# A four-layer vision tower: routed tiles in two 64-row halves with an expert each, and wide attention with its values through DRAM

## What is computed

```
# wide attention, on rms_norm(x, norm1_w)
qkv = x @ w_qkv                        # 12 + 3 + 3 heads of 64
q = apply_rope(q, cos, sin); k = apply_rope(k, cos, sin)
scores = jnp.einsum('bhqd,bhkd->bhqk', q, k) / jnp.sqrt(jnp.float32(HD))
attn = jax.nn.softmax(jnp.where(causal, scores, min), axis=-1)
out = jnp.einsum('bhqk,bhkd->bhqd', attn, v) ... @ w_out

# top-2 routed part, E = 16, FF = 384
vals, idx = jax.lax.top_k(jax.nn.softmax(x2d @ w_router, axis=-1), 2)
vals = vals / jnp.sum(vals, axis=-1, keepdims=True)
for e in range(E):
    gate, up = jnp.split(x2d @ w_gate_up[e], 2, axis=-1)
    out = out + combine[:, e:e + 1] * ((silu(gate) * up) @ w_down[e])

# top-1 routed part, 4 experts, H = 768
top = jnp.argmax(x @ Wg + bg, axis=-1)
y = gelu(x @ W1[top] + b1[top]) @ W2[top] + b2[top]
```

## Time and the profile before

| | |
|---|---|
| time, median of three executions (lowest to highest) | 876.16 us (874.68 to 876.18) |
| the profiled execution: time, span, granted clock | 874.83 us, 873.0 us, 0.977 |
| wide attention | 123 to 262 us |
| first routed part: plan and the last weights | 270 to 302 us |
| its tiles | 302.4 to 437.6 us |
| top-1 tiles | 800.6 to 864 us |

### The profile page before, as it was taken

One profiled execution on the slowest core, in us unless ns is written; L12 is line 12 of the kernel. 1 busy time (PEld: TensorE's weight loads), 2 busy tenths in 40 slices (PEclk: granted clock), 3 DMA queues, 4 the chain that ended last, 5 costly groups with the idle time before them and its releaser, 6 DMA issues. The chain is left out here.

```text
span 873.0 us, 16411 instructions
## 1 busy us (share of the span) xinstructions
PE 814.8 (93%) x5930; PEld 583.5 (67%) x5931; DVE 421.1 (48%) x891; ACT 352.8 (40%) x785; POOL 189.9 (22%) x209
## 2 busy tenths in 40 slices
PE   6999989999999899999999879999999999998997
PEld 4666666677775467777658556765678577665775
DVE  5576577788725322222249677772003477722011
ACT  2375544464332023332325665443241545423332
POOL 0561113554400134444300002000000200001332
PEclk9999999999979999999999999999999999989999
DMA  9021100000005877212133001664000055403110
GB/s 314 1 41 26 17 2 1 1 2 1 2 1 157 230 186 206 59 45 47 40 101 90 0 1 31 134 148 127 1 1 1 11 87 109 115 2 113 45 52 31
DMA packets 80141, 56.21 MB, mean 64 GB/s; under 512 B 53254, under 2 KB 73256, under 8 KB 80076
## 3 DMA queue, kind: packets, MB, share of 16 engines
q1 hardware_dynamic: 71644, 41.26, 19.7%
q0 software_dynamic: 4416, 9.84, 4.1%
q10 hardware_dynamic: 4016, 4.23, 1.5%
HBM read 45.96 MB, written 9.35 MB: 63 GB/s over the span
## 5 line engine op out<-in xcount | busy, mean ns | idle before, releaser
L79 PE MATMUL banks<-con 128*128 128x512 f32 (+1 forms) x230 | 103.6, 566 | 3.0 <-DVEq L2268 1.4
L1978 PE MATMUL banks<-moe_wu,moe_xf 96*128 x256 | 89.1, 492 | 1.7 <-ACT moe_xf L2086 0.9
L1978 PEld LDWEIGHTS banks<-moe_wu,moe_xf 96*128 96x128 f32 x256 | 46.0, 189 | 30.0 <-issue 2.2
L79 PEld LDWEIGHTS banks<-con 128*128 128x128 f32 x230 | 43.5, 203 | 31.8 <-issue 28.4
L154 ACT ACTIVATE ln_sq<-x 96x544 f32<-96x544 f32 x32 | 21.0, 656 | 86.3 <-DVE x L146 86.2
L2283 DVE TENSOR_TENSOR moe_hid<-banks,moe_gs 128x384 f32<-128x384 f32 x32 | 17.9, 558 | 76.2 <-PE banks L1978 76.2
L688 PE MATMUL banks<-x,a_wqkv 96*96 96x272 f32 x192 | 48.0, 395 | 0.0
L2140 POOL DMA_INDIRECT moe_xs<-moe_x_rows,moe_taken x32 | 31.4, 981 | 74.8 <-PE banks L1962 53.0
L1216 DVE TENSOR_TENSOR a_kx<-a_k,con 96x1632 f32<-96x1632 f32 x21 | 38.7, 1850 | 8.0 <-ACT a_k L993 7.7
L1181 POOL MEMSET a_q<- 96x60 f32 x3 | 0.4, 147 | 181.8 <-POOLq L2566 91.9
L164 PE MATMUL banks<-ln_sq,con 96*96 96x272 f32 x128 | 35.6, 400 | 4.0 <-ACT ln_sq L154 3.9
(11 more groups left out here) (413 smaller groups left out, 1720.0 us busy)
## 6 DMA issues: line engine op xcount, KB each, us to landing
moe_wu<-in_moe_up SPq DMA_DIRECT2D x16, 576.0 KB, 11.7
f_w<-in_f_e SPq DMA_DIRECT2D x10, 576.0 KB, 8.2
moe_wd<-in_moe_down SPq DMA_DIRECT2D x16, 288.0 KB, 13.0
patch_px<-in_patches SPq DMA_DIRECT2D x4, 768.0 KB, 9.5
a_vt<-a_v_rows SPq DMA_DIRECT2D x72, 36.0 KB
a_v_rows<-a_vtok SPq DMA_DIRECT2D x24, 96.0 KB, 2.1
f_wu<-in_f_up SPq DMA_DIRECT2D x4, 576.0 KB
f_wd<-in_f_down SPq DMA_DIRECT2D x4, 576.0 KB
```

The lines of the kernel that those rows point to most:

```text
L79: self.nc.tensor.matmul(self.ps[bank][:, 0:width], self.ident, self.con[:, 0:width], start=True, stop=True)
L1978: last = nc.tensor.matmul(ps[2 + 2 * p + u][:, 0:BW], xf[0:KU[a], p, a], wu[0:KU[a], bass.ds(e, 1), a, u * BW:(u + 1) * BW].rearrange("p e ...
```

## The change

**Tiles in two halves.** Counts are rounded up to 64 rows (HT), and a tile consists of two 64-row halves, each with its own expert: `tile_expert` has two entries for each tile, and there are 25 tiles in top-2 and 10 in top-1. Each up and down product becomes two products of 64 rows: rows 0 to 63 go by the first half's expert, in place, rows 64 to 127 by a copy of the second half's weights, `up_copy` and `down_copy`, two of each, made by DVE (96x1536 and 128x576 float32; in top-1 97x1536 and 128x1152). In top-2 the copies lie in the room of `env.x` and `env.x2`, now declared 128 partitions wide. TensorE's `up` waits for `up_copied`, `down` for `down_copied`. DVE's `copy_up(i)` reads the expert number, waits for `w_ready` and for the up products of tile i - 2. In top-1, `take_row` becomes two instructions of 64 rows. The rest of the loop is as before, with 128 rows.

**Values through DRAM.** The two value steps of `project` (L1479) become one that makes the values by token: two blocks of 128 tokens by 192 columns, and for the last 16 tokens a block of 32 rows by 96 columns, twice. ScalarE moves them in two pieces to `vtok`; SyncE writes them to `v_rows` in DRAM (four transfers a chunk) and reads them back as `vt` (three a chunk), 18 rows by 16 images by 64 for each head, of which the 18th row has its slot only. `turn_values`, `take_values` and `vs` are gone; NT = 10.

**Router products spread.** In the last chunk the products of `route_early` for one tile stand behind each of the steps 0 to 3 of the first group; of the remaining two, one stands ahead of each of the steps 0 and 1 of the second group. Their waits move ahead of the first group's steps.

```diff
+HT = 64
+MOE_TILES = -(-((2 * T + NE * (HT - 1)) // HT) // 2)
+TOP1_TILES = -(-((T + NX * (HT - 1)) // HT) // 2)
...
-    NT = TQK + 2
+    NT = TQK + 1
...
+            def write_values(c):
+                sp.wait_ge(taken, NT * (c + 1))
+                for u in range(2):
+                    sp.dma_start(v_rows[c, 128 * u:128 * (u + 1)], vtok[:, c % 2, u * D:(u + 1) * D]).then_inc(v_written, 16)
...
+            def read_values(c):
+                sp.wait_ge(v_written, 64 * (c + 1))
+                if c >= 2:
+                    sp.wait_ge(filled, fill_of(GPC * (c - 1) - 1, 5) + 1)
...
                 else:
-                    w, at, rows = (wv, 0, 2 * WD) if t == TQK else (wv, 2 * WD, WD)
...
+                    for u in range(2):
+                        for a in range(2):
+                            nc.tensor.matmul(to[:, u * D:(u + 1) * D], chunk(x2, c)[:, a, 128 * u:128 * (u + 1)], wv[:, a], start=a == 0, stop=a == 1)
+                    for a in range(2):
+                        for m in range(2):
+                            last = nc.tensor.matmul(to[SLOT * m:SLOT * (m + 1), 2 * D:2 * D + HD], chunk(x2, c)[:, a, CW - SLOT:CW],
+                                                    wv[:, a, m * HD:(m + 1) * HD], start=a == 0, stop=a == 1)
...
+                if not more:
+                    pe.wait_ge(router.small_in, 16)
+                    pe.wait_ge(n2.ready, 2 * (c - 1))
                 for u in range(6):
                     weigh(2 * c, u)
                     if more:
                         project(c + 1, 2 + u)
+                    elif u < ROUTED:
+                        env.route_early(pe, router, x2, 0, u, u + 1)
                 if not more:
-                    pe.wait_ge(router.small_in, 16)
                     pe.wait_ge(n2.ready, 2 * c)
-                    env.route_early(pe, router, x2, 0, 0, EARLY)
                 for u in range(6):
+                    if not more and ROUTED + u < EARLY:
+                        env.route_early(pe, router, x2, 0, ROUTED + u, ROUTED + u + 1)
                     weigh(2 * c + 1, u)
...
             def up(i, p):
                 e = expert(i)
                 pe.wait_ge(w_ready, e + 1)
                 pe.wait_ge(x_moved, i + 1)
+                pe.wait_ge(up_copied, i + 1)
...
                     for a in range(2):
-                        last = nc.tensor.matmul(ps[2 + 2 * p + u][:, 0:BW], xf[0:KU[a], p, a],
-                                                wu[0:KU[a], bass.ds(e, 1), a, u * BW:(u + 1) * BW].rearrange("p e f -> p (e f)"),
-                                                start=a == 0, stop=a == 1)
+                        nc.tensor.matmul(ps[2 + 2 * p + u][0:HT, 0:BW], xf[0:KU[a], p, a, 0:HT],
+                                         wu[0:KU[a], bass.ds(e, 1), a, u * BW:(u + 1) * BW].rearrange("p e f -> p (e f)"),
+                                         start=a == 0, stop=a == 1)
+                        last = nc.tensor.matmul(ps[2 + 2 * p + u][HT:RT, 0:BW], xf[0:KU[a], p, a, HT:RT],
+                                                up_copy[p][0:KU[a], a, u * BW:(u + 1) * BW], start=a == 0, stop=a == 1)
...
+            def copy_up(i, p):
+                e = expert(i, 1)
+                dve.wait_ge(w_ready, e + 1)
+                wait(dve, up_ready, i * 2 - 2)
+                V.tensor_copy(up_copy[p], wu[0:KU[0], bass.ds(e, 1)].rearrange("p e a f -> p (e a) f")).then_inc(up_copied, 1)
+
+            def copy_down(i, p):
+                e = expert(i, 1)
+                V.tensor_copy(down_copy[p], wd[:, bass.ds(e, 1)].rearrange("p e j d -> p (e j) d")).then_inc(down_copied, 1)
...
             def body(i, p, ahead):
                 if top2 and ahead >= 1:
                     gate(i + 1, 1 - p)
+                if ahead >= 2:
+                    copy_up(i + 2, p)
                 if not isinstance(i, int) or i >= 1:
                     move_y(i - 1, 1 - p)
+                if ahead >= 1:
+                    copy_down(i + 1, 1 - p)
                 if not top2 and ahead >= 2:
                     take_row(i + 2, p)
```

More of the change, by code:

```diff
@@ L1499, in bank, with weigh @@
                 return ps[6 + n % 2]
-            def turn_values(g):
+            def weigh(g, u):
                 c = g // GPC
-                pe.wait_ge(taken, NT * (c + 1))
-                to = bank(g, 0)
-                for i in range(GI):
-                    last = nc.tensor.transpose(to[0:KS, i * WD:(i + 1) * WD],
-                                               vs[:, c % 2, (g % GPC) * GI + i].rearrange("p g k -> p (g k)"), env.ident[0:WD, 0:WD])
-                last.then_inc(filled, 1)
-            def weigh(g, u):
                 if u == 0:
@@ L1841, in stage_routed_ffn @@
             here = spare[:, K * NR * LISTS * TL:K * NR * (LISTS + 1) * TL].rearrange("p (k t i) -> p k t i", k=K, t=NR)
+            room = [w[:].rearrange("p a t -> p (a t)") for w in env.whole]
+            up_copy = [r[0:HD, 0:2 * FN2].rearrange("p (a f) -> p a f", a=2) for r in room]
+            down_copy = [r[:, 2 * FN2:2 * FN2 + NH * D].rearrange("p (j d) -> p j d", d=D) for r in room]
+            tile_cmp = spare[0:1, K * NR * LISTS * TL:K * NR * LISTS * TL + 2 * TL * E].rearrange("p (i e) -> p i e", e=E)
             at_lane = experts.wd[:, E - 4:E].rearrange("p e j d -> p (e j d)").rearrange("p (k t r) -> p k t r", k=K, t=NR)
@@ L1844, in stage_routed_ffn @@
             bg, b2 = router.bg, router.b2
-            rest = sb("rest", [RT, TL, D])
+            up_copies, down_copies = sb("up_copies", [KU[0], 2, 2, FN2]), sb("down_copies", [128, 2, NH, D])
+            up_copy, down_copy = ([w[:, p] for p in range(2)] for w in (up_copies, down_copies))
+            rest, tile_cmp = sb("rest", [RT, TL, D]), sb("tile_cmp", [1, 2 * TL, E])[:]
             listed, here, at_lane = sb("listed", [RT, K, NR, LISTS, TL]), sb("here", [RT, K, NR, TL]), sb("at_lane", [RT, K, NR, RT])
@@ L1878, in tiles_loop @@
                 body(i, i, 2)
-            with eng.Fori(1, TL // 2 - 2) as it:
+            turns = (TL - 3) // 2
+            with eng.Fori(1, turns) as it:
                 for u in range(2):
                     body(it * 2 + u, u, 2)
-            for i in range(TL - 4, TL):
+            for i in range(2 * turns, TL):
                 body(i, i % 2, min(2, TL - 1 - i))
@@ L2032, in _ @@
             tiles_loop(pe, body)
-            down(TL - 1, 1)
+            down(TL - 1, END)
             if norm_out:
@@ L2308, in _ @@
             tiles_loop(dve, body)
-            move_y(TL - 1, 1)
+            move_y(TL - 1, END)
             def sum_rows(b):
```

128 lines of the change are left out of this document (67 added, 61 removed).

## The result

The changed kernel took **854.97 us** in the median of four executions (849.39 to 856.25), the one before 875.83 (874.68 to 876.18). The ratio is 0.9752 with a 95% interval of 0.9706 to 0.9798. The forecast was 854, with a range of 843 to 872. In a later session on another chip six executions stood at 851.37 to 852.22, at a ratio of 0.9709 (0.9669 to 0.9749). The profiled execution took 856.25 us, span 854.4, clock 0.977; so the two profiles differ by 18.6 us of span, the medians by 20.9.

What follows compares the result with a forecast made beforehand. TensorE, busy 814.8 of 873.0 us, was taken as the bound, with VectorE bounding the changed top-2 loop. Terms -5.7, -8.4, -4.8 and -3.0 sum to -21.9: 874.8 becomes 852.9, on the median's scale 854; range 843 to 872.

Steps and rivals of the forecast that it cites:

- Top-2 tile over VectorE's chain: Top-2 loop: up products, gate, expert-number read, copy, next up products bound a tile at 5.22 us; -5.7 us.
- Halves side by side, 0.25 us a stay: Up and down products: 64-column halves run together at the present rate, plus 0.25 us per stay in half width.
- The copy waits for the gather: Rival, top-2 loop: the up copy cannot run beside POOL's gather, 0.71 us later per tile; 16.3 us more, 870; chance 0.30.
- Early copy: Rival, top-2 loop: expert number read under the gate, copy starts at the gate's end; 11.3 us less, 843; chance 0.13.
- slow copy: Rival, both routed loops: the up copy takes 1.74 us instead of 0.95; 879 us, slower than before; chance 0.05.
- halves in turn: Rival, routed loops: half-width products run one after the other, up products double; about 110 us more, 964; chance 0.03.
- Top-1: Top-1 loop: 10 tiles of 5.68 us for 12 of 5.43, copies hidden with 0.6 us to spare; -8.4 us.
- Attention before the last chunk: Wide attention: value transposes (4.4 us) and one filler (0.4) go, values through DRAM arrive in time; -4.8 us.
- Last chunk: Wide attention's end: spread router products gain 6.0 us if the clock stays up, 0.9 if it falls; middle taken, -3 us.

Runs made afterwards that it cites:

- routed stages alone: The changed kernel's routed stages with the wide attention of the kernel before; 858.1 us, ratio 0.9794 to the kernel before.
- changed kernel again: The changed kernel as it is, in six more executions in the later session; 851.82 us.
- router products in one piece: Changed kernel with the six router tiles in one piece between the last chunk's groups, as before the change; 857.43 us against 851.82.
- early copy: Changed kernel with the up copy of tile i + 3 behind the scaling of tile i - 1, in both routed stages; 838.71 us, ratio 0.9568.
- half a copy: Changed kernel with only the first of two parts of the up weights copied in top-2 (96x768); 841.63 us, ratio 0.9624.
- the two with fillers: Filler products around the norm's products of chunk 0: in the changed kernel 850.84 us against 851.82; together with the earlier up copy 834.94 us.

## Why the prediction was right, step by step

The forecast held in time and in its largest mechanism, the chain over the copy. That the sum came so near is in part luck. In the pair of profiles attention before the last chunk gave 4.2 us less than its term, the places without a term cost 2.8, and top-1 gave 1.2 less; the last chunk gave 3.7 more and top-2 1.1 more. The median of 854.97 beside 854 is luck too: six executions of the same kernel in the later session stand at 851.82.

- **Top-2 tile over VectorE's chain: right.** The parts were 2.92, 1.05, 0.95 and 0.30, and measured 2.85, 1.02, 0.96 and 0.20; 5.22 against 5.03 us. The term was 5.7, and 6.8 came, a loop of 128.3 us where the forecast had 129.5. Of the 128.3, 1.7 are a piece at half clock in the first tiles, from 297 to 300; in the profiles of the routed stages alone, of the changed kernel again and of the router products in one piece the same loop takes 126.6 to 126.7. By 23 x 0.19 less it should be 125.1. The rest lies in how the sum was set up: the tiles before alternate between 4.11 and 4.19 us, 4.15 in the mean, so outside of them there were 2.3 us and not 1.1; and the last two tiles take 5.18 and 5.12. The runs with an early copy and with half a copy show that it is this chain and no other: 4.40 and 4.63 us.
- **Halves side by side, 0.25 us a stay: right.** Eight slots of 384 columns take as long as eight full records, and TensorE's own tile is 4.40, which is 0.25 more than the mean of 4.15 before; the forecast had 4.44.
- **The copy waits for the gather (rival, 0.30): didn't come, but its rule was half right.** The gather starts 0.10 or 0.11 us before the copy in 19 of the 21 tiles of the loop that have both. The copy took its 0.96 all the same; the gather took 1.18 instead of 0.98. The Trainium skill, SBUF — State Buffer, "Who interferes with whom", says that a copy in a two-port mode and a GpSimd instruction exclude each other, and that the one issued first holds the ports for the whole instruction. The trace agrees that they get in each other's way. It does not agree on who waits: the gather came first, and it is the gather that ended later, 0.12 us after the copy's end. That was hidden. The rival's 16 us came from the assumption that a gather holds what the copy needs from its start on.
- **Early copy, slow copy, halves in turn: each refuted by a row of the tile above** (copy 1.02 us after the gate; 0.96; slots of 0.32).
- **Top-1: the size was off, and so was its cover.** The forecast was 5.68 a tile and no stall. Of the seven tiles behind the first two, five took 5.71 to 5.87 and two 6.22 and 6.42. (The first two tiles together took 7.2 us up to the third's up products, as in the kernel before, so nothing is lost there.) In the tile shown the copy starts 4.36 us behind the output sum, where the forecast had 3.52 (+3.8 less +0.28). It counted 0.8 us from the down copy to the first half of the rest and again to the second, though its own rows gave 0.92 to 1.10 for a read and its operation; 1.09 and 1.21 were measured. In all the copy is 0.84 us late, more than the 0.6 us to spare. The tile of 6.42 waits for no copy but for TensorE's own read of an expert number, and the run with the early copy has four tiles of that kind; the forecast had no term for it. The term was -8.4 and gave -7.2.
- **Attention before the last chunk: the step that failed.** The term was -4.8, the profile shows -0.6. The forecast treated the clock in the last chunk only and didn't consider the half clock in chunk 0. What that costs can be read from the profile of the half copy, which has the same attention and in this stretch a clock of 1.00. Its stretch from the first projection to the last chunk's first weighing stands second here, that of the kernel before first:

```profile
123.96:242.46 118.50, 112.99 (x913) 84.28 (x913) 90.35 (x186) 54.13 (x118) 55.89 (x68) 1.00 0.01 1
122.86:238.25 115.39, 107.87 (x879) 81.96 (x880) 89.09 (x185) 47.56 (x106) 56.37 (x68) 1.00 0.06 16
```

The changed kernel's own profile has 117.9 us for it, so the half clock cost 2.5. The other 1.7 of the missing 4.2 are idle time. TensorE's work fell by 5.1 us, a little more than forecast, but its idle time rose by 2.0, from 5.5 to 7.5: waits that the value transposes used to cover. The groups of this stretch before (the last column is the idle time and its cause):

```profile
L1491 PE MATMUL banks<-g_k,g_q 64*102 64x51 f32 x256 | 13.2, 252 | 0.0
L1516 PE MATMUL banks<-con,g_p 102*96 102x102 f32 x96 | 12.7, 253 | 0.0
L1524 PE MATMUL banks<-g_pt,g_vt 96*64 96x102 f32 x192 | 10.4, 255 | 0.3
...
L1506 PE MATMUL banks<-con,g_vs 64*96 64x64 f32 x64 | 4.9, 215 | 0.0
```

and after:

```profile
L1519 PE MATMUL banks<-g_k,g_q 64*102 64x51 f32 x256 | 13.2, 252 | 0.2 <-DVE g_s L1736 0.2
L1536 PE MATMUL banks<-con,g_p 102*96 102x102 f32 x96 | 13.1, 268 | 0.5 <-DVE g_p L1751 0.5
L1546 PE MATMUL banks<-g_pt,g_vt 96*64 96x102 f32 x192 | 10.4, 255 | 1.1 <-ACT g_pt L1636 1.1
```

The 4.9 us of transposes (L1506) are gone, and in front of the scores, the transposes of the probabilities and the products with the values 0.2, 0.5 and 1.1 us of idle stand, where 0.3 stood. They end with VectorE's and ScalarE's work; none is put down to the transfers of the values through DRAM. A removed cover should have been costed so: name what the next product waits for.
- **Last chunk: middle taken, upper end came, with its parts mis-sized.** It gave 6.7 us, where 6.0 was the end for a clock that stays up. The mixed steps let the clock fall in one profile of seven, the piece in three of three. Before and after, from the first weighing to the end of the output projection:

```profile
242.46:265.24 22.78, 21.38 (x146) 16.83 (x145) 3.53 (x7) 6.65 (x13) 0.00 (x0) 0.70 0.00 1
241.87:257.97 16.10, 14.80 (x145) 12.37 (x144) 4.42 (x8) 6.71 (x13) 0.00 (x0) 1.00 0.00 1
```

TensorE's busy time fell by 6.6 us and its idle time by 0.1, from 1.4 to 1.3. The forecast had 0.9 us hidden in idle time, and 2.3 + 2.8 for the clock. So the hiding, the only part of the term that did not hang on the clock, all but failed, and the clock gave all the rest.
- **Outside the parts: +2.8 us that no term held.** Of the 2.0 us between the loops 1.7 is again the clock: the shares below 1.00 add up to 6.8 us lost there before and 8.5 after. The cause of the 0.8 in the plan is open.

So the sum of 21.9 stands against 18.5 in the pair of profiles and 20.9 in the medians. Without the half clock in chunk 0 the pair would have some 21.0.

## What to carry to other kernels

Where a change puts a copy between an engine's product and its next one, write the chain once round from trace rows (product, handover, queue, copy, handover) and compare it with the bound engine's own work; if the chain is longer, look first for another place in the order, since here that alone was worth 14 us in the loop, with the same buffers. Where work goes that nothing needed, its neighbours' waits come out from under it. Narrow products in one piece went with the half clock in three profiles of three here, the same products spread between denser ones in one of seven; the gain lies in the products that follow, which run at full clock. And look for half-clock pieces before and after in every stage, not only where the change aims at them: here they moved, and a single pair of profiles put 2.5 us too little down to attention.

## What the runs showed of the hardware

- A one-input copy on VectorE can hold up an indirect DMA's instruction on GpSimd (0.98 us alone). Where the copy began up to 0.5 us after it and outlasted its first 0.9 us, the instruction ended 0.12 or 0.13 us after the copy, in both loops: 1.18 us under a copy that ends at +1.06, 1.50 under one that ends at +1.38, 1.42 to 1.45 under one that ends at +1.30 to +1.33, 1.86 and 2.05 where a second copy followed that ended at +1.74 and +1.93. Where the copy had begun 0.05 us or more ahead of it, and no other followed under it, it ended 0.82 to 0.87 us after the copy's end (1.74 us, copy until +0.89). A copy over at +0.66 cost it nothing. The copies keep their 0.96 us there. Where a copy began late, 0.63 or 0.64 us after the instruction, it was the copy that took some 0.15 us longer (1.11 for 0.96, 0.91 for 0.76) and the instruction kept its 0.99. All this fits a conflict at the instruction's start and near its end alone; that reading is inferred from these times.
- The copy's cost is not proportional: 0.96 us for 1536 elements a partition, 0.56 for 768, 0.46 for 576 on 128 partitions, 0.76 for 1152.
- The half clock in chunk 0 is not settled by what TensorE does ahead of it. In the changed kernel's profile TensorE is busy 1.73 of the 3 us from 147 to 150, and the clock falls behind them. In all six profiles of the changed attention without fillers the same stretch of the program has the same 1.72 or 1.73 us of work (in that of the half copy the stage begins 1.1 us earlier, and the stretch is 145.89 to 148.89). Behind it the clock was lost for 1.7 us in one, 3.4 in three, about 10 in one, and not at all in the sixth. In the two profiles with the attention of before, with 2.21 us of work in the stretch, and in the two with fillers, with 2.89, it did not fall. So the piece came in five of six profiles with the thin stretch and in none of four with a fuller one; what else decides whether it comes and how long it is stays open.
